# Staging queries and keys through DRAM in the order of the operand stacks: one transfer per kind and group instead of six

## The reference

```
q, k, v = heads(h @ Wqkv + b)          # (2, 16, 1024, 16) each
scores  = q @ k^T * 16 ** -0.5
x       = x + (softmax(scores) @ v) @ Wo + bo
```

## Time and profile before

| | |
|---|---|
| median of 3 runs | 4522.99 us (4517.64 to 4530.47) |
| the profiled execution | 4537.6 us, its span 4535.8 us |
| TensorE (PE) busy | 4070.6 us, 90% |
| VectorE (DVE), ScalarE (ACT), GpSimd (POOL) busy | 66%, 46%, 30% |
| DMA, mean share of 16 engines | 27.9% on the queue that SP issues on |
| narrow layers | from the start to about 1536 us of the span |

### The profile page before, as it was taken

One profiled execution on the slowest core, in us unless ns is written; L12 is line 12 of the kernel. 1 busy time (PEld: TensorE's weight loads), 2 busy tenths in 40 slices (PEclk: granted clock), 3 DMA queues, 4 the chain that ended last, 5 costly groups with the idle time before them and its releaser, 6 DMA issues.

```text
span 4535.8 us, 55477 instructions
## 1 busy us (share of the span) xinstructions
PE 4070.6 (90%) x20428; PEld 2486.0 (55%) x20428; DVE 3010.2 (66%) x4405; ACT 2076.4 (46%) x3756; POOL 1349.6 (30%) x664
## 2 busy tenths in 40 slices
PE   7999979799998888998999967888999999997889
PEld 5343357634335675555555545666555555546668
DVE  5888755688885666777777844345677777764355
ACT  2656645255564543443444435553444344435541
POOL 1100011100001035655555543321444444441120
PEclk8999989899998999999999978998999999998999
DMA  4223230312323142331333222323232222214220
GB/s 131 39 43 49 44 70 24 56 30 43 47 44 63 32 88 63 66 65 39 65 66 66 63 65 67 70 61 63 69 70 60 67 66 66 60 47 108 68 54 20
DMA packets 151983, 269.28 MB, mean 59 GB/s; under 512 B 34090, under 2 KB 67812, under 8 KB 150688
## 3 DMA queue, kind: packets, MB, share of 16 engines
q1 hardware_dynamic: 151712, 265.72, 27.9%
HBM read 105.01 MB, written 29.64 MB: 30 GB/s over the span
## 4 chain that ended last, share of the span: by engine, by line
PE 38%; DVE 8%; ACT 4%; POOL 4%; issue 4%; SPq 3%; DMA 1%; POOLq 0%; DVEq 0%; ACTq 0%
PE PS L1015 19%; PE PS L1194 7%; PE PS L1087 4%; PE PS L1236 4%; PE PS L1324 2%; DVE t L1757 2%; SPq L2173 2%; ACT t L1490 1%; DVE PS L1829 1%; SPq L2190 1%; POOL t L2035 1%; PE PS L1118 1%; POOL t L2022 1%; POOL t L2008 1%; PE PS L1204 1%
## 5 line engine op out<-in xcount | busy, mean ns | idle before, releaser
L1015 PE MATMUL PS<-t 128*128 128x512 f32 (+4 forms) x7896 | 1988.9, 384 | 160.4 <-ACT t L1469 24.8
L1469 ACT ACTIVATE t<-PS 128x512 f32<-128x512 f32 (+2 forms) x1600 | 1166.9, 750 | 1124.7 <-PE PS L1015 1118.3
L1015 PEld LDWEIGHTS PS<-t 128*128 128x128 f32 (+2 forms) x7896 | 1253.8, 188 | 708.9 <-issue 253.5
L1194 PE MATMUL PS<-t 128*32 128x512 f32 (+2 forms) x4352 | 809.7, 610 | 0.2
L1757 DVE TENSOR_REDUCE t<-PS 128x1 fp32r<-128x1024 f32 x512 | 622.0, 1220 | 281.4 <-PE PS L1087 275.8
L1761 DVE TENSOR_REDUCE t<-PS 128x1 f32<-128x512 f32 x1024 | 651.4, 684 | 73.1 <-PE PS L1091 70.7
L2035 POOL TENSOR_TENSOR t<-t 128x1024 f32<-128x1024 f32 x256 | 617.6, 2412 | 133.6 <-ACT t L1469 106.9
L1091 PE MATMUL PS<-t 96*128 96x512 bf16 x1024 | 370.3, 394 | 34.8 <-DVE t L1761 14.3
L1087 PE MATMUL PS<-t 128*128 128x512 f32 x1024 | 339.9, 415 | 58.8 <-DVE t L1757 36.4
L2031 POOL TENSOR_TENSOR t<-t 128x1024 f32<-128x1024 f32 x64 | 155.0, 2422 | 734.4 <-PE PS L1204 442.1
L1194 PEld LDWEIGHTS PS<-t 128*32 128x32 f32 (+2 forms) x4352 | 170.7, 122 | 329.1 <-issue 324.4
(11 more groups left out here) (131 smaller groups left out, 3804.9 us busy)
## 6 DMA issues: line engine op xcount, KB each, us to landing
t<-t SPq DMA_DIRECT2D x640, 128.0 KB, 2.5
t<-scr_n SPq DMA_DIRECT2D x288, 128.0 KB, 6.4
t<-t SPq DMA_DIRECT2D x128, 256.0 KB, 3.8
scr_n<-t SPq DMA_DIRECT2D x72, 256.0 KB, 2.3
t<-t SPq DMA_DIRECT2D x256, 64.0 KB, 2.0
t<-in_L_Wg SPq DMA_DIRECT2D x16, 768.0 KB, 4.6
t<-in_L_W SPq DMA_DIRECT2D x36, 256.0 KB, 3.2
t<-in_L_Wo SPq DMA_DIRECT2D x64, 128.0 KB, 2.5
```

Of the source, the lines that this page charges most:

```text
L1015: ins = e.matmul(out, l, r, start=i == 0, stop=i == len(terms) - 1, tile_position=tp)
L1194: ins = e.matmul(banks[S.ot][wd * j:wd * j + wd, :], u.v[j][kt], P[0:S.pr, j, :], start=kt == 0, stop=kt == S.nkt - 1, tile_position=(0, w ...
L1469: e.activation(dst, src, ACT.Exp, scale=S.L.scale).then_inc(*expd.inc((S.i, i)))
```

## The change

`scr_n` gets another shape: [b, qk, 16 heads, 96 rows, 1024], so that the 96 rows of a head's stack stand in it in their final order. `keep16` writes a part once for each slot that it fills: 6 DMAs per kind and chunk instead of 3, so 12 instead of 6 in self-attention and 6 instead of 3 in cross-attention, each still 256 KB. Their DRAM side is 8 heads by 16 rows by 1024 now, no longer 128 rows in a line. `stack16` reads a group with one DMA of 768 KB per kind, 96 partitions by 4 heads by 1024: two instead of twelve in self-attention, one instead of six in cross-attention. Over the four stages concerned the writes go from 72 to 144 DMAs and the reads from 288 to 48.

Beside this, `NMX` becomes two tiles that alternate by unit (the padding behind shrinks by the same amount), with a wait of DVE on its own `mjoin` of two units before; and in the rope layer the `kstack` and `qstack` steps wait for both halves of the turned operand rather than for the second.

```diff
+G6 = (G6Q, G6K)
...
-    NATD = dram("scr_n", (NB, 2, 3, 256, N), BF16)
+    STKD = dram("scr_n", (NB, 2, 16, 96, N), BF16)
...
-            S.NMX = sbt(c, [128, 16, 2])
+            S.NMX = [sbt(c, [128, 16, 2]) for _ in range(2)]
...
-            sbt(c, [128, 976])
+            sbt(c, [128, 944])
...
+                if m >= 2:
+                    w.wait_ge(max_part, (S.i, m - 2))
...
-                        e.dma_start(NATD[b, qk, part, 128 * ch:128 * ch + 128, :], S.NAT[:, ch, 3 * qk + part, :]
-                                    ).then_inc(*nat_kept[ch].inc((S.i, b), 16))
+                        for slot in [i for i in range(6) if G6[qk][i] == part]:
+                            e.dma_start(STKD[b, qk, 8 * ch:8 * ch + 8, 16 * slot:16 * slot + 16, :],
+                                        S.NAT[:, ch, 3 * qk + part, :]).then_inc(*nat_kept[ch].inc((S.i, b), 16))
...
-                for s in range(6):
-                    for qk in range(S.nqk):
-                        src = NATD[g // 4, qk, (G6Q, G6K)[qk][s], 64 * (g % 4):64 * (g % 4) + 64, :].rearrange("(h r) n -> r h n", r=16)
-                        e.dma_start(S.QK[g % S.nbuf][16 * s:16 * s + 16, qk, :, :], src
-                                    ).then_inc(*stacked[g % S.nbuf].inc((S.i, g), 16))
+                for qk in range(S.nqk):
+                    src = STKD[g // 4, qk, 4 * (g % 4):4 * (g % 4) + 4, 0:96, :].rearrange("h r n -> r h n")
+                    e.dma_start(S.QK[g % S.nbuf][0:96, qk, :, :], src).then_inc(*stacked[g % S.nbuf].inc((S.i, g), 16))
...
-                    w.wait_ge(nat_low, (S.i, rope_order(S).index((S, g, qk, 1))))
+                    for half in range(2):
+                        w.wait_ge(nat_low, (S.i, rope_order(S).index((S, g, qk, half))))
```

More of the change, by code:

```diff
@@ L1759, in vector_program @@
                     continue
+                if m >= 2:
+                    w.wait_ge(max_part, (S.i, m - 2))
                 o, k, nth = full(w, ("max", S.i, m, j, qt, half))
-                e.tensor_reduce(S.NMX[:, 4 * j + qt, half:half + 1], o, AX.X, ALU.max).then_inc(*bank_free[k].nth(nth))
+                e.tensor_reduce(S.NMX[m % 2][:, 4 * j + qt, half:half + 1], o, AX.X, ALU.max).then_inc(*bank_free[k].nth(nth))
             elif what == "cmax":
@@ L1775, in vector_program @@
                     w.wait_ge(bank_free[k], nth)
-                e.tensor_reduce(S.MT[m % 2][:, 0:n], S.NMX[:, 0:n, :], AX.X, ALU.max, negate=True
+                e.tensor_reduce(S.MT[m % 2][:, 0:n], S.NMX[m % 2][:, 0:n, :], AX.X, ALU.max, negate=True
                                 ).then_inc(*max_part.inc((S.i, m)))
```

## The result

| | before | after |
|---|---|---|
| median | 4525.44 us (4517.64 to 4535.87, 20 runs) | 4536.02 us (4525.45 to 4543.03, 20 runs) |
| profiled execution | 4537.6 us | 4535.6 us |

The account below looks back on a forecast made before the run. PE is busy 90% of the span, so narrow-layer transfers count only where PE stalls, 20 us in sum. Terms 18 + 17 + 11 + 14.5 + 4 + 4 = 68.5 us, put on the median: 4591 us, 1.5% slower; range 4518 to 4620.

Parts of the forecast that it names:

- the price of a write: Each 256 KB blocked write of keep16: eight engines at half pace, 101 GB/s, 2.6 us; twelve take 31 us of queue.
- rival (A): Writes use eight engines at full pace, 1.3 us each; about 0 us in sum, 4523 us; chance 0.12.
- layer 0 start: Twelve writes, then the stack, put the stack at 94.2 against a first max at 75.75: +18 us.
- layer 0 cross-attention: Both chunks' writes and two groups' reads delay the row of maxima to 668.3 against 656.98: +11 us.
- layer 1 start: Twelve writes, then the stack, put the stack at 879.6 against 862.54: +17 us.
- layer 1 cross-attention: The writes and reads delay the row of maxima to 1473.3 against 1458.71: +14.5 us.
- The four exposed places: Starts and cross-attentions of layers 0 and 1, where PE waits on transfers: +18, +17, +11 and +14.5 us.
- mid self-attention: In layers 0 and 1, a row of maxima waits behind nine writes, to 240.7 instead of 237: +4 us each.
- the second chunk's writes: At the layer starts they queue behind stack reads and end about when the first row of maxima is issued: nothing.
- The reads: Two transfers onto 96 partitions at 220 GB/s: a stack takes 9.1 us instead of 15.1, 6 us gained wherever exposed.
- The small edits: NMX with its DVE wait, and the rope waits: nothing.
- Layers 2 and 3: Expected unchanged, as a sign that the forecast was right.

Follow-up runs that it names:

- Run 7: The changed kernel with a write's DRAM side as four padded blocks of 32 rows, stacks read in two parts, slots innermost: 4615.83 us, ratio 1.0206.
- Run 8: The kernel with slots innermost (0.9963), the cross-attentions' last stack reads issued one step later, behind the row of maxima: 4501.48 us, ratio 0.9954.
- the square of runs: Old or new reads, plain or blocked writes, equal write counts: old/plain 1.0015, new/plain (slots innermost) 0.9963, old/blocked 1.0073, new/blocked (the change) 1.0022.
- run 5: The kernel before with the small edits alone (two tiles for the maxima, the rope layer's two waits): 4521.79 us, ratio 0.9998.
- run 3: The kernel before with each part written as often as the change does, as plain rows, extra copies to an unread tensor: 4528.34 us, ratio 1.0015.
- run 1: The changed kernel with slots innermost in scr_n, so a write's DRAM side is 128 strided rows; same bytes and DMA counts: 4504.57 us, ratio 0.9963.

## Why the prediction was wrong

**The step that failed is the price of a write**: "I take 2.6". The number of engines in it was right (share 0.53); that they would run at half pace, "because blocks of 16 neighbouring partitions meet as the 32-partition copies do", was wrong. They ran at 25.5 GB/s each, and the write took 1.28 us, the price of rival (A). I had carried over the slowness of transfers that have all 16 engines on 16 or 32 partitions. For the eight-block write the second of the prices I named, eight engines at the single pace of 25.6 GB/s, was the right one. Only the first 1.6 us of a burst show anything like what I feared (51 and 26 GB/s). The trace of before had a warning. I priced the 77-partition copy by one window, 184 GB/s at a share of 0.70. The next such copy, issued at 3063.53, shows this:

```profile
3064.80:3065.00 0.20, 0.20 (x4) 0.20 (x3) 0.00 (x0) 0.20 (x2) 0.20 (x1) 1.00 0.56 205
```

That is 205 / (0.56 x 16) = 22.9 GB/s for each engine's worth of busy time, against 410 / (1.08 x 16) = 23.7 in plain rows and 204 / (0.53 x 16) = 24.1 in the eight-block writes. In the window that I used it is 184 / (0.70 x 16) = 16.4. So even before the result the rows on fewer engines disagreed, and one of them stood near full pace.

As to the Trainium skill's page "SBUF — State Buffer" ("Door 1: The DMA port swizzle"), my estimate from it was eight engines on four ports, 2.4 us; a burst that runs at 204 GB/s for six microseconds doesn't bear that estimate out. The remark that the 16-partition reads agree with four ports was loose as well: four ports at its 27 GB/s make 108, and the reads moved 120.

**The rest of the sum, tested at its own price.** Run 7 has the price that I took, so its drifts can be set against the terms of the forecast (its reads are other ones, in two parts and from slots innermost). From the same landmarks as above, in us:

| place | forecast | run 7 | change |
|---|---|---|---|
| layer 0 start | 18 | 19.5 | 4.0 |
| layer 0 self-attention | 4 | 18.5 | 2.0 |
| layer 0 cross-attention | 11 | 12.7 | 2.0 |
| layer 1 start | 17 | 17.9 | 4.0 |
| layer 1 self-attention | 4 | 7.0 | -3.0 |
| layer 1 cross-attention | 14.5 | 16.5 | 3.1 |
| sum | 68.5 | 92.1 | 12.2 |

The four exposed places come out within 2 us each: the places and the mechanism were right. What is left over lies inside the self-attentions, at two places of run 7 (two windows of writes, then reads; then two stretches of its timeline):

```profile
263.00:264.00 1.00, 0.00 (x0) 0.00 (x0) 0.25 (x1) 0.00 (x0) 0.00 (x0) 1.00 0.27 104
266.00:267.00 1.00, 0.00 (x0) 0.00 (x0) 0.00 (x0) 0.00 (x0) 0.00 (x0) 0.50 1.02 373
...
256.98 6.35 SPq L2148 DMA_DIRECT2D t<-t  x4
263.37 1.93 SPq L2131 DMA_DIRECT2D t<-scr_n  x4
...
198.47 4.50 POOL L1975 TENSOR_TENSOR t<-t 128x2048 f32<-128x2048 f32 x1 [62.19 <-DMA t<-in_rows]
198.49 5.03 DVE L1663 TENSOR_TENSOR t<-t 128x512 fp32r<-128x512 f32 x1
204.17 0.61 PE L1092 MATMUL PS<-t 96*128 96x512 bf16 x1 [4.60 <-DVE t L1764]
```

The term "mid self-attention", 4 us, was mis-sized: 10.2 us go at the second entry's first chunk in layer 0, and 10.4 in layer 1. I had let the row of maxima land 0.5 us behind the writes. The writes run at about 102 GB/s until some 264.2, and the row is issued by 263.33, yet PE gets it only at 270.54, after waiting 8.39 us (shown with run 7). In between the engines move 1.75 MB at up to 373 GB/s; the stack issued behind the row, at 263.37, is 1.57 MB. So the row came about when the stack behind it was through. Layer 1 repeats it: a wait of 8.60 us until 1106.87. The rest is the granted clock, 0.50 in the windows from 266 to 274.

The other place is 7.6 us in the first units of layer 0, between the row copies at 124.64 and 221.31. It isn't the second chunk's writes, for which I had put "nothing": at 189.78 the drift has grown by only 0.6 us. The other 7 come behind that. One subtraction on DVE takes 5.03 us where the other three of its line take 0.69, as all four do in every other kernel; it starts 0.02 us after a 4.50 us addition on POOL. PE waits 4.60 us and then works at a granted clock of 0.50 to about 211. This belongs to how that one kernel's steps fell, and no term of the sum stands for it. In layer 1 the same units stand 3.7 us ahead of before's, by the slow stretch of before's profile named above, which is why that row of the table shows 7.0 and not 10.

At the price that the writes really have, the mid term is nothing, as rival (A) said: the change's drift is 4.4 and 4.5 us on its two sides in layer 0 (226.97, 260.54 before), 8.0 and 8.0 in layer 1.

**Rival (A)** had the right price, and gave about 0. Its own steps against the change: layer 0 start +3 (measured 4.0), layer 1 start +1.5 (4.0), cross-attention -4 and 0 (2.0 and 3.1). At the starts the 1.6 us of slow running ahead of each burst (51, 56, 26 and 77 GB/s from 847.20 to 848.80) is what it lacked for the most part. In layer 0's cross-attention its end of the writes, 644.9, was right: about 651.5, less the 6.5 us by which this stage begins later. But from there to the row of maxima it took 8.3 us and it took 12.7 (to 664.20), with these windows between:

```profile
652.00:654.00 2.00, 1.64 (x14) 0.61 (x13) 0.69 (x1) 0.73 (x2) 0.00 (x0) 1.00 0.97 345
654.00:656.00 2.00, 0.00 (x0) 0.00 (x0) 0.00 (x0) 0.36 (x1) 0.00 (x0) 1.00 1.07 265
656.00:658.00 2.00, 0.00 (x0) 0.00 (x0) 0.00 (x0) 0.00 (x0) 0.00 (x0) 0.59 1.06 229
```

At 230 to 345 GB/s some 3 MB move in that time, and the two stacks and the load of 256 KB ahead of the row are 1.83 MB. So transfers issued behind the row were served before it was through, as in run 7. Run 8 fits that only in part, since it takes away bytes ahead of the row: with a stack less there, the wait is gone. No run takes away those behind it, and why the row is passed wasn't tried.

**The reads**: right. 220 GB/s taken, 249 measured with PE idle; "a stack takes 9.1 us instead of 15.1" came out at 8.8 and 8.7. That they are worth something only where exposed is right too; the square of runs gives 24 us in all. **The small edits**: nothing, by run 5. **Layers 2 and 3**: no effect shown.

That the measured 4536 us lies between 4518 and 4620 was owed to rival (A), whom the range was drawn to take in, and not to the sum.

**The gain that the change could have had** was lost to its doubled bytes only for 7 us (run 3). It was lost to the form of the writes: 27 us. Before and after look alike because -24 and +34 nearly cancel.

## What to carry to other kernels

Look at both sides of a DMA, and at the outermost size of each: eight blocks on one side halve a 128-row write to 204 GB/s, and the same bytes with the small index innermost ran at 388. When no row shows the new form of a transfer, take the number of engines and the pace of one engine as two separate guesses, and put a slowdown on the second only if rows show it at that number of engines, over more than one window. And before writing data twice to make reads cheap, try the partitions: spreading each slot over every sixth one took 120 GB/s to 203, and more than half of the gain, at no extra byte.

## What the runs showed of the hardware that I had not expected

- A burst of blocked writes starts slowly, the more so the fewer the blocks. With eight it moved 26 to 108 GB/s from 53.40 to 54.60 (windows of the result), with sixteen it was at 174 GB/s in the window at 53.80, and with four blocks at 20 and 15 GB/s from 54.20 to 55.00. Plain rows ran at 410 from the first. The share meanwhile is 0.27 to 0.64 with eight blocks, out of proportion to what moves. It was so at 211.8, 636.0 and 847.2 too, where the engines had been idle, but writes queued behind reads ran at 205 GB/s from 79.20 on, right behind them. Why wasn't tried.
- The issue of a DMA took the longer, the slower the transfers in the queue: the median for a 256 KB write was 0.34 us with six plain writes at a time, 0.46 with twelve strided ones (run 1), 0.61 with sixteen blocks, 1.17 with eight and 2.34 with four, close to the time that the write itself takes in the last two. A slow transfer so holds up SP's whole program, and the small row copies behind it: the four issued at 256.98 in run 7 took 6.35 us, against 2.44 at the same place before.
- A DMA into 16 partitions costs SP 0.60 us to issue when they are strided, and 0.43 when they are neighbours.
- A DVE subtraction of 0.69 us took 5.03 when it began beside a 4.50 us addition on POOL (run 7, 198.49). In the changed kernel the same addition begins at 183.71, just as the last of these subtractions (183.2) has nearly ended, and nothing is lost. Why it took longer wasn't tried.
